# Rewritten front of a routed attention block: x in both layouts, statistics without GpSimd, logits as columns of the attn_w product, rows normalised in the expert loop

## The reference

```python
# x: (16, 256, 128)
qkv = x @ W_qkv + b_qkv;  q, k, v = split(qkv)
attn = softmax(q @ k.T / sqrt(128));  x = x + (attn @ v) @ W_out + b_out
x = layernorm(x)                                    # no gain, no bias, eps 1e-5

h = x + layer_norm(x, ln1_g, ln1_b) @ attn_w.T
t = layer_norm(h, ln2_g, ln2_b)
logits = t @ gate_w.T;  top_vals, top_idx = top_k(logits, 2);  rw = softmax(top_vals)
for e in range(8):                                  # gate_proj, up_proj: 512 x 128
    out += comb[:, e] * ((silu(t @ gate_proj[e].T) * (t @ up_proj[e].T)) @ down_proj[e].T)
x = layernorm(x' + h + out)                         # x' is the block's input
```

## Time and profile before

| | |
|---|---|
| median of three runs | 405.9 us |
| span of the profiled execution | 403.7 us, 9351 instructions |
| busy in the span: TensorE | 309.9 us (77%) |
| VectorE | 287.6 us (71%) |
| ScalarE | 189.6 us (47%) |
| GpSimd | 210.4 us (52%) |
| activation table loads | 2, of 1283 ns |

### The profile page before, as it was taken

The page is one execution under the profiler, slowest core; times in us unless marked ns, Lnnn a source line. Parts: engine busy times, 40 slices in busy tenths (PEclk is TensorE's granted clock), DMA queues, the critical chain, the costliest instruction groups (busy, mean ns, idle before and its releaser), DMA issues.

```text
span 403.7 us, 9351 instructions
## 1 busy us (share of the span) xinstructions
PE 309.9 (77%) x2041; PEld 268.2 (66%) x2042; DVE 287.6 (71%) x1108; ACT 189.6 (47%) x474; POOL 210.4 (52%) x276
## 2 busy tenths in 40 slices
PE   3999888888765204999999999999999999970000
PEld 2788777776544103888888898988888898860000
DVE  2589999999998725766666666666666666634992
ACT  3887757677643202444444434344443434420552
POOL 0031888788787785243434343444434444354992
PEclk9999999999975555999999999999999999995555
DMA  6610111144511131112111111111111111105871
GB/s 200 198 52 26 42 63 57 54 145 151 198 35 41 47 94 25 41 39 56 42 52 39 52 41 45 50 40 52 39 52 41 45 50 39 42 12 156 213 205 53
DMA packets 33853, 29.52 MB, mean 73 GB/s; under 512 B 4753, under 2 KB 31381, under 8 KB 33696
## 3 DMA queue, kind: packets, MB, share of 16 engines
q1 hardware_dynamic: 24576, 18.36, 16.3%
q0 software_dynamic: 4320, 8.47, 6.1%
q10 hardware_dynamic: 4928, 2.36, 2.0%
HBM read 18.02 MB, written 11.61 MB: 73 GB/s over the span
## 4 chain that ended last, share of the span: by engine, by line
PE 54%; DVE 29%; issue 7%; DMA 4%; POOL 3%; ACT 2%; SPq 0%; DVEq 0%; ACTq 0%; POOLq 0%
PE bank L503 15%; PE bank L465 8%; PE bank L467 8%; PE bank L466 8%; PE bank L493 8%; DVE y L715 2%; DVE rows L673 2%; PE bank L476 2%; DVE x_all L873 2%; POOL expert_rows L913 2%; DVE n L658 2%; DVE st L754 1%; DVE st L721 1%; DVE topi L780 1%; DVE w_lo L769 1%
## 5 line engine op out<-in xcount | busy, mean ns | idle before, releaser
L963 POOL DMA_INDIRECT moe_rows<-ysb,idx x71 | 71.3, 1005 | 35.6 <-issue 18.5
L503 PE MATMUL bank<-wd,hidT 128*128 x568 | 75.4, 276 | 0.7 <-ACT ysb L608 0.6
L913 POOL DMA_INDIRECT expert_rows<-rows,place x64 | 63.4, 990 | 17.9 <-issue 13.9
L859 DVE SCALAR_TENSOR_TENSOR hid<-sg,xrow,bank 128x512 f32<-128x512 f32 x71 | 53.1, 748 | 24.2 <-PE bank L467 22.5
L503 PEld LDWEIGHTS bank<-wd,hidT 128*128 128x128 f32 x568 | 69.0, 192 | 1.4 <-issue 1.3
L608 ACT ACTIVATE ysb<-bank 128x128 f32<-128x128 f32 x71 | 19.8, 278 | 102.6 <-PE bank L503 102.6
L465 PE MATMUL bank<-w_hi,t_hi 128*128 x142 | 62.2, 438 | 3.8 <-DVE t_lo L851 3.8
L959 POOL TENSOR_TENSOR idx<-xrow,zero_i 128x1 int32<-128x1 int32 x71 | 12.7, 180 | 86.9 <-issue 56.9
L849 DVE CAST t_hi<-t 128x128 fp32r<-128x128 f32 x71 | 19.9, 281 | 51.8 <-ACT t L595 51.8
L467 PE MATMUL bank<-w_hi,t_lo 128*128 x142 | 56.5, 398 | 0.0
L466 PE MATMUL bank<-w_lo,t_hi 128*128 x142 | 56.2, 396 | 0.0
(11 more groups left out here) (122 smaller groups left out, 592.7 us busy)
## 6 DMA issues: line engine op xcount, KB each, us to landing
xrow<-expert_rows SPq DMA_DIRECT2D x71, 65.0 KB, 1.8
w_raw<-weights SPq DMA_DIRECT2D x16, 256.0 KB, 3.9
yin<-moe_rows SPq DMA_DIRECT2D x16, 256.0 KB, 3.8
xin<-x SPq DMA_DIRECT2D x16, 128.0 KB, 2.2
wd<-weights SPq DMA_DIRECT2D x1, 2048.0 KB, 9.2
out<-x_all ACTq DMA_DIRECT2D x16, 128.0 KB, 3.3
moe_rows<-ysb,idx POOLq DMA_INDIRECT x71, 2.4
expert_rows<-rows,place POOLq DMA_INDIRECT x64, 2.3
```

Of the source, the lines that this page charges most:

```text
L503: last = mm(banks[7][:, 0:P], hidT[i2][:, c * P:(c + 1) * P], wd[:, bass.ds(w + c * P, P)], start=(c == 0), stop=(c == NC - 1))
L859: V.scalar_tensor_tensor(hid[i2][:, :], sg[i2][:, :], xrow[r1][:, D:D + 1], banks[2 + i2][:, :], ALU.mult, ALU.mult).then_inc(sm["hid_done ...
L913: G.indirect_dma_start(out=expert_rows[:, :], out_offset=bass.IndirectOffsetOnAxis(ap=place[b % NR][:, t, k:k + 1], axis=0), in_=rows[b % ...
L963: G.indirect_dma_start(out=moe_rows[:, :], out_offset=bass.IndirectOffsetOnAxis(ap=idx[r3][:, :], axis=0), in_=ysb[r3][:, :], in_offset=No ...
```

## The change

The front is rewritten, the two other stages only adapted.

- The host gives x twice, as it was and transposed, so the transposition of x on TensorE and its copy on ScalarE go. Loads of x are fewer and larger.
- The bias of v goes in through a product of ones with a matrix that holds the bias in three bf16 parts; ScalarE instead of VectorE copies v out. A column of ones in `vo` makes the product with v give the softmax sum, so the accumulator reads go.
- Batches are handled in groups: [0], [1, 2], [3, 4], ..., [13, 14], [15]. In steady state the first norm and the routing of a group are in an odd step, h and its statistics in an even step.
- GpSimd computes no powers in the front. ScalarE gives exp(-0.5 ln v) as a first value and VectorE makes one Newton step (`half`, `corr`, `r`), for both norms.
- `wa` is a matrix of 144 columns, worked out at the start: attn_w with the gain, the mean's removal and the bias folded in, then gate_w and attn_w times gate_w. One product with the transposed x1 gives the update of h and both parts of the logits. The n1 rows, the transposition of the second normalised rows and the logits product go.
- The table in memory holds h not normalised, with mean, inverse root, weight and destination (132 columns instead of 130). A transfer of SyncE copies each row for its second expert. In the expert loop VectorE normalises (`tn`) before the transposition, and every later operation moves one step on: the loop's depth is 4 instead of 3.
- The single addition of x1 and h on GpSimd is cut into 64 additions of 64 columns inside the expert loop.

The core of the diff:

```diff
@@ ScalarE, front
-                    for t in range(NT):
-                        A(prob[b % 2][:, t, :], ps_s[:, t * S:(t + 1) * S], ACT.Exp,
-                          bias=negmax[b % 2][:, t:t + 1], accum_out=rsum[b % 3][:, t:t + 1]
+                if g_v is not None:
+                    g, n = g_v, count(g_v)
+                    act.wait_ge(sm["v0_done"], 2 * g + 2)
+                    A(ln0[g % 2][:, :, 0:n], v0[g % 2][:, :, 0:n], ACT.Ln).then_inc(sm["ln0_done"], 1)
+                    act.wait_ge(sm["ln0_done"], g + 1)
+                    A(seed0[g % 2][:, :, 0:n], ln0[g % 2][:, :, 0:n], ACT.Exp, scale=-0.5).then_inc(sm["seed0_done"], 1)
...
+                if g_n is not None:
+                    act.wait_ge(sm["v2_done"], g + 1)
+                    A(ln2[g % 2][:, 0:n], v2[g % 2][:, 0:n], ACT.Ln).then_inc(sm["ln2_done"], 1)
+                    act.wait_ge(sm["ln2_done"], g + 1)
+                    A(seed2[g % 2][:, 0:n], ln2[g % 2][:, 0:n], ACT.Exp, scale=-0.5).then_inc(sm["seed2_done"], 1)
@@ VectorE, front
-                    for t in range(NT):
-                        V.tensor_scalar(n1[b % 2][:, t, :], y[b % 2][:, t, :], mv0[b % 2][:, t, 0:1],
-                                        rs0[b % 2][:, 1, t:t + 1], ALU.subtract, ALU.mult).then_inc(sm["n1_done"], 1)
-                    V.tensor_tensor(flat(vo[b % 3]), ps_v, flat(bias_out), ALU.add).then_inc(sm["v_sb"], 1)
+                    dve.wait_ge(sm["seed0_done"], g + 1)
+                    V.scalar_tensor_tensor(half0[:, :, 0:n], v0[g % 2][:, :, 0:n], -0.5, seed0[g % 2][:, :, 0:n],
+                                           ALU.mult, ALU.mult).then_inc(sm["half0_done"], 1)
...
+                            V.scalar_tensor_tensor(rows[:, k, 0, 0:D], ps_a[side(b)][:, t, 0:D],
+                                                   ratio[g % 2][:, k - first:k - first + 1], xs[:, b, t, :],
+                                                   ALU.mult, ALU.add).then_inc(sm["h_done"], 1)
@@ TensorE, front
-                        last = mm(ps_l[:, t, :], tT[b % 2][:, tok(t)], params[:, GW:GW + E], start=True, stop=True)
+                            last = mm(ps_a[side(b)][:, t, :], nT[g_n % 2][:, tok(j)], wa[:, :], start=True, stop=True)
+                    pe.wait_ge(sm["member_done"], g_r + 1)
@@ GpSimd
-                    G.tensor_tensor(rs2[b % 2][:, :], var2[b % 2][:, :], mhalf[:, 0:NT], ALU.pow
-                                    ).then_inc(sm["rs2_done"], 1)
-            G.tensor_tensor(whole(x1_all), whole(x1_all), whole(h_all), ALU.add).then_inc(sm["res_done"], 1)
             def experts(s, r, live):
-                if live(3):
-                    pool.wait_ge(sm["idx_done"], s - 2)
-                    pool.wait_ge(sm["ysb_done"], s - 2)
+                if live(4):
+                    pool.wait_ge(sm["idx_done"], s - 3)
+                    pool.wait_ge(sm["ysb_done"], s - 3)
                 if live(1):
                     i, r1 = s - 1, (r - 1) % RING
                     pool.wait_ge(xr_in[r1], turn(i, r1))
                     if far(i, RING):
                         pool.wait_ge(y_sent[r1], turn(i, r1) - 16)
...
-                if live(3):
-                    r3 = (r - 3) % RING
+                if live(4):
+                    r4 = r % RING
                     G.indirect_dma_start(
...
+                if not isinstance(s, int) or s < 2 * TOKEN_TILES:
+                    G.tensor_tensor(xs_flat[:, bass.ds(s * RES, RES)], xs_flat[:, bass.ds(s * RES, RES)],
+                                    rows_flat[:, bass.ds(s * ROW + (r % 2) * RES, RES)], ALU.add
@@ VectorE, expert loop
+                    V.tensor_scalar(tn[r % 2][:, :], xrow[r][:, 0:D], xrow[r][:, C_MEAN:C_MEAN + 1],
+                                    xrow[r][:, C_R:C_R + 1], ALU.subtract, ALU.mult).then_inc(sm["tn_done"], 1)
```

More of the change, by code:

```diff
@@ L153, in block_kernel @@
[L153 to L162 removed]
+        mv0 = ring("mv0", [P, GT, 2])
+        v0 = ring("v0", [P, 2, GT])
@@ new lines, in block_kernel @@
+        half2 = sb("half2", [P, GT])
+        corr2 = sb("corr2", [P, GT])
+        za = sb("za", [P, GT, E])
+        zb = sb("zb", [P, GT, E])
+        zc = sb("zc", [P, GT, E])
+        lg = sb("lg", [P, GT, E])
+        top = sb("top", [P, GT, 8])
+        topi = sb("topi", [P, GT, 8], U32)
+        onehot = sb("onehot", [P, GT, TOPK, E])
+        member = ring("member", [P, GT, E], BF16)
+        base = sb("base", [P, E])
+        slots = sb("slots", [P, GT, E])
+        picked = sb("picked", [P, GT, TOPK, E])
@@ L164, in block_kernel @@
+        place = sb("place", [P, TOKEN_TILES, TOPK], I32)
+        gap = ring("gap", [P, GT])
+        ex = ring("ex", [P, GT])
+        exp1 = sb("exp1", [P, GT])
         cnt = sb("cnt", [1, E])
@@ L190, in block_kernel @@
         t_lo = ring("t_lo", [P, P], F32R)
-        sg = ring("sg", [P, INTER])
-        hid = ring("hid", [P, INTER])
+        sg = [a[:, :, :].rearrange("p t k -> p (t k)") for a in prob]
+        hid = [a[:, :, :].rearrange("p t k -> p (t k)") for a in probT]
         hidT = ring("hidT", [P, INTER])
@@ new lines, in block_kernel, with ps_logits, tiles, count @@
+        ps_n = banks[5][:, :]
+        side = lambda b: (b + 1) % 2
+        ps_a = [pair[:, i, 0:NT * A_COLS].rearrange("p (t c) -> p t c", t=NT) for i in range(2)]
+        def ps_logits(g, at):
+            bs = GROUPS[g]
+            i = side(bs[0])
+            wide = pair[:, i:i + len(bs), 0:NT * A_COLS].rearrange("p b (t c) -> p b t c", t=NT)
+            return wide[:, :, :, at:at + E]
+        def tiles(g):
+            return slice(NT * GROUPS[g][0], NT * GROUPS[g][-1] + NT)
+        def count(g):
+            return NT * len(GROUPS[g])
@@ new lines, in values @@
+            def values(b):
+                if b >= 1:
+                    pe.wait_ge(sm["v_sb"], b)
+                ranked = sum(1 for last in ENDS_AT if last + 5 < b)
+                if ranked:
+                    pe.wait_ge(sm["base_done"], ranked)
+                mm(ps_v, ones[:, :], bias_split[:, :, :], start=True, stop=False)
+                for t in range(NT):
+                    last = mm(ps_v[:, t, :], xT[:, b, tok(t)], wvo[:, :], start=False, stop=(t == NT - 1))
+                last.then_inc(sm["v_ps"], 1)
@@ L366, in front @@
+                if g_n is not None:
+                    if g_n >= 1:
+                        pe.wait_ge(sm["n1T_sb"], g_n)
+                    else:
+                        pe.wait_ge(sm["wa_ready"], 1)
+                    for j in range(count(g_n)):
+                        pe.wait_ge(sm["x1_done"], tiles(g_n).start + j + 1)
+                        last = nc.tensor.transpose(ps_n[:, tok(j)], xs_tile(tiles(g_n).start + j), ident)
+                    last.then_inc(sm["n1T_ps"], 1)
                 if live(2):
@@ new lines, in front @@
+                if live(0) and s >= 1:
+                    qk(s)
+                    values(s)
+                if s == 2:
+                    pe.wait_ge(sm["waT_sb"], 1)
+                    mm(banks[5][:, 256 + D:256 + D + E], wa_T[:, :], wa[:, D:D + E], start=True, stop=True
+                       ).then_inc(sm["gate_ps"], 1)
+                if g_r is not None:
+                    m, n = member[g_r % 2], count(g_r)
+                    pe.wait_ge(sm["member_done"], g_r + 1)
+                    pe.wait_ge(sm["v_sb"], min(s + 1, B))
+                    if g_r >= 1:
+                        pe.wait_ge(sm["base_done"], g_r)
+                    for t in range(n):
+                        for u in range(t):
+                            mm(ps_r[:, t, :], ones[:, :], m[:, u, :], start=(u == 0), stop=False)
+                        mm(ps_r[:, t, :], tri[:, :], m[:, t, :], start=(t == 0), stop=True)
+                    for t in range(n):
+                        last = mm(ps_t, ones[:, :], m[:, t, :], start=(t == 0), stop=(t == n - 1))
+                    last.then_inc(sm["t_ps"], 1)
@@ new lines, in front @@
+                if live(0) and s >= 1:
+                    query_key(s)
+                    values(s)
+                if g_v is not None:
+                    g = g_v
+                    act.wait_ge(sm["shift0_done"], g + 1)
+                    act.wait_ge(sm["y_done"], tiles(g).stop)
+                    act.wait_ge(sm["r0_done"], g + 1)
+                    for j in range(count(g)):
+                        at = xs_tile(tiles(g).start + j)
+                        A(at, at, ACT.Identity, bias=shift0[g % 2][:, j:j + 1], scale=r0[g % 2][:, 0, j:j + 1]
+                          ).then_inc(sm["x1_done"], 1)
```

901 lines of the change are left out of this document (466 added, 435 removed).

## The result

The changed kernel takes 473.1 us (median of 4 runs, 471.4 to 474.4) against 406.6 us for the kernel before in the same series: 1.164 times as long, 95% interval 1.160 to 1.168. The forecast was 454.8 us, range 422 to 480, slower with 0.93. The profiled execution has a span of 469.5 us, 65.8 over that of before.

The account below looks back on a forecast made before the run. VectorE bounded the front before; table loads in a round of waits would bound it after. Span 403.7 + 32.3 (to the first gate product) + 16.6 (expert loop) = 452.6, so 454.8 us measured, range 422 to 480.

Parts of the forecast that it names:

- The front's mechanism: Front: four table loads per two steps stand on the path through ScalarE, TensorE and VectorE; 8.6 us a batch against 7.0.
- The walk through the round: Front: following one two-batch period through VectorE, TensorE and ScalarE from the first norm's Exp gives 17.2 us.
- Price of a load: ScalarE in the front: 1.28 us per table load, bound 1.78, four in two batches, 34 more than before.
- Clock: TensorE in the front: clock falls to 1.2 GHz in each gap, adding 1.4 us for a period of 18.6.
- Tail: Front's end: step 17's Exp at 148.1, last row scatter at 182.8, first gate product 7.0 later at 189.9.
- Pitch: Expert loop: idx waits for the scatter just issued; 3.1 us per tile (2.80 to 3.34), 67 intervals; loop 16.6 longer.
- Three last tiles: End of the expert loop: three scatter intervals of 1.7 us when nothing waits.
- ScalarE is fed without waits: Rival, front: ScalarE's sum of 13.7 rules; first gate product at 159, time between 407 and 424; chance 0.12.
- The scatter lands early enough: Rival, expert loop: minimum landing of 2.1, so only the front pays: 438; chance 0.15.
- Half clock through the whole front: Rival, TensorE: 22.3 us a period, first gate product at 212, time 477; chance 0.13.
- The loads hide: Rival, front: loads hidden or absent, VectorE's 11.8 rules each pair; first gate product at 148, time 396; chance 0.05.
- VectorE's relief: Front: VectorE's work for two batches falls to 11.8 us against 13.9, the odd step holding some 7.2.

Follow-up runs that it names:

- the three edits together: Changed kernel with one table set for Ln and Exp, scatter ahead of idx, and the second row copy by ScalarE: 405.2 us on chip 8.
- the filler: Changed kernel with 24 more TensorE products before each of six rank products: 462.0 us on chip 8, 1.135 to 1.143 of the kernel before.
- the three and 12 products: Changed kernel with one table set, scatter ahead of idx, copy by ScalarE and 12 products before each of six rank products: 425.0 us (chip 1), 400.9 (chip 7).
- the four on chip 0: Changed kernel with one table set, 460.0 us; scatter ahead of idx, 449.7; wd load two steps later, 480.4; all three edits, 430.1.

## Why the prediction was right, and where it was off

**The front's mechanism: right.** The loads stand in a round through all three engines and aren't hidden. On chip 0 taking out the loads alone shortens the first two periods by 5.2 and 4.1 us; on chip 8 the three edits together give back 37 us ahead of the first output scatter, where the change had lost 36.5 in the first trace. The walk through the round gave 17.2 us at full clock; the run with the clock kept full has 16.9. That the forecast of 18.6 meets the mean of the five full periods, 18.58, so closely is luck: the walk is 0.3 too long and the price of the clock about as much too low.

**Price of a load: right at 1.28.** Their number was two short. The 1.78 of the bound isn't there: 0.01 us from a load's end to the next activation. Neither is the drain of about 1.38 us that the Trainium skill gives in "ScalarE: Activation LUTs", section "What ACT_TABLE_LOAD costs": ahead of a load there are 0.02 to 0.03 us. The Trainium skill's section "Table sets: the hidden batching unit" on the same page has Ln and Exp in one set. That does hold here, but only when the program asks for that set: two loads then, and 38 in the compiled program, which reloads at each change.

**Clock: right, a little low.** 1.4 us a period was the forecast, 1.5 to 2.1 is what the filler gave back. The clock was down where the products began again behind the 6 us gap, and full again 4.1 us later, within the 2.4 to 4.4 drawn from the earlier trace rows.

**Tail: 3 us short.** Step 17's Exp came at 149.8 for 148.1: step 5's was 1.9 late (40.4 for 38.5), and the six periods add up to 109.4 us for 109.6. From there the chain was 1.1 longer, 0.6 of it the wait for the last weight piece, which the prediction had left out. t_hi did lose its 3.7 us: last row scatter to first gate product took 7.3 for 7.0. From there to the first output scatter it was 10.0 for 8.8, the clock's later rise.

**Pitch: the step that was mis-sized.** The prediction took 2.4 + 0.64 + 0.06 = 3.1 and kept 3.34 as the upper bound. The trace's landings and starts give, over 67 tiles, a median of 2.49 from a scatter's start to its landing, 0.16 from the landing to idx's start, and 0.65 from idx to the next scatter: 3.30, and 3.31 was measured. So landing and wake are each about 0.1 over what the prediction took (2.4 and 0.06). Over 67 intervals the 0.21 are 14.1 of the 16.9 us by which the span was missed. The pair shown above, with 2.79 from the scatter at 262.60 to its idx, is one of the longer: its landing took 2.63. The 3.34 of the upper bound lies nearer to 3.31, but by chance: it took the 0.3 that GpSimd needs behind ysb, and behind a landing it needs half of that.

**Three last tiles: 1.3 us too dear.** 1.28 us each, not 1.7.

**Rivals.** "ScalarE is fed without waits" falls: it idles 17.2 us for nT alone. "The scatter lands early enough" falls with the pitch. "Half clock through the whole front": 0.80 on average, and full from 103 us to 107 in the pair shown. "The loads hide" falls. Its number for VectorE's relief was sound: the terms of the odd step add up to 7.6 and not 7.2, but VectorE's busy time is 68.4 us in the six periods from 40.4 to 149.8, 11.4 a pair against the 11.8. That number rules no pair even without loads: a pair then takes 13.0 to 14.4 us, and TensorE's products and ScalarE's copies stand in the chain beside VectorE.

## What to carry to other kernels

Count table loads in the compiled order, not activations in the source: 36 loads of 1.28 us, most of them in a round of three engines, cost about 37 us, the whole loss of the rewritten front (22 us on the chip with late increments). When a ring's depth stays and its last stage moves back by one, look at what waits for the slot: it may now wait for the transfer just issued, and the cure was the order of two lines. For such a wait of GpSimd on a transfer, charge its median landing and 0.16 us of wake.

## What the runs showed of the hardware

- On chips 0 and 1 TensorE's increments reached VectorE and ScalarE 4 to 5 us late, four times in each trace of the new front (seven kernels ran there; one has the front of before). Four or five increments of TensorE then stand 0.06 us apart: at each of the four places in five of these traces, at two in the sixth (the three and 12 products), and nowhere in the front of any trace of chips 7 and 8, of the first two, or of the old front on chip 1. In every trace of chips 0 and 1 semaphore events are missing: 4,953 to 5,879 are recorded, against 6,897 to 7,049 in those of the others and the two first traces. With the new front the missing events and the lateness go together; which makes which, and whether an execution without recording has the lateness, stays open. The kernel with the old front on chip 1 lacks events too (5,731) but shows no such wait: its last row scatter is at 148.7, for 147.2 in the first trace. The kernel before took 407 to 410 us on these two chips and 406 to 407 on the others; the one program with the new front that ran on both kinds took 24 us more. Why the old front escapes wasn't found.
- A difference between chips of 6% of the time in one kernel and under 1.2% in another means that only kernels of one chip can be compared. My first reading of the four on chip 0, made against a trace of another chip, would have charged the edits with it.
- A load of the activation tables, 1283 ns here, has nothing beside it: 0.01 us to the next activation, 0.02 to 0.03 from the one ahead.
- GpSimd started an instruction 0.16 us (median) after the landing it waited for, and 0.30 after ScalarE's ysb.
